# In a linear-attention loop, ScalarE scales the fourth output tile one step later and rounds phi between relu and exponential

## The chip, the core and the metric

One Trainium2 chip, one core. The metric is the device time of one execution of the program, in microseconds (us). Below, PE is the matmul engine (TensorE), DVE is VectorE, ACT is ScalarE, POOL is GpSimd, and SP issues the transfers (DMA) between device memory and on-chip memory.

## The reference, cut to what matters

Six stages act on x (4 sequences of 1024 tokens, 256 features): quantised linear layer, linear attention, quantised linear layer, routed MLP, softmax attention, routed MLP. Only the second is touched:

```python
q = hidden_states @ Wq.T + bq        # 16 heads of 128
k = hidden_states @ Wk.T + bk        # 4 key heads
v = hidden_states @ Wv.T + bv
sq = elu_plus_one(q)                 # phi
sk = elu_plus_one(k)
kv = jnp.einsum('bhsd,bhse->bhde', sk, v)
qkv = jnp.einsum('bhsd,bhde->bhse', sq, kv)
k_sum = sk.sum(axis=2)
norm = jnp.einsum('bhsd,bhd->bhs', sq, k_sum)
attn = qkv / (norm[..., None] + EPS)
return attn @ Wo.T                   # added to x
```

## The kernel before, in words

`linear_attention_phase` first folds kv and Wo of a head into one matrix `m` (128 x 258: 256 output features, then the key sum). Then its loop takes one step `t` for each half sequence (512 tokens, `CH`) of each head: 32 steps (`LOOP`) a sequence, 128 in all, with 16 steps ahead of them for the keys of the first sequence. Every fp32 product is made of three matmuls of rounded parts, high x high, high x low, low x high (`split3`, lines 35 to 37), so each operand exists as a high part, rounded by ACT, and a low part, the difference, made by DVE or POOL.

A query step `t` runs so. PE makes the query of step t (six matmuls of 512 columns) in a bank of PSUM. ACT takes relu(-(q + bias)) (line 1210) and exp(-that) (line 1213); DVE joins both to phi in `f[:, t % 2]` (line 1320, below "the query step of DVE"). In step t + 1 ACT rounds phi into `ph` (line 1202) and POOL makes the low part `pl` (line 1142). In step t + 2 (`LAG` = 2) PE makes the four output tiles of 128 tokens (twelve matmuls of 258 columns), ACT copies their norm columns (line 1219), DVE takes the reciprocal `rnorm` (line 1328) and adds three scaled tiles into x (line 1332), ACT scales the fourth into `ybuf` (line 1239), and POOL adds it to x in the step after (line 1148).

Each engine runs one written list, step by step, and only semaphores tie the lists together. ACT's list in a step before the change: round phi of t - 1; evict the results of step t - 1 (`evict`, `act_evict`); relu and exponential of t; norm columns; key part (lines 1224, 1226, 1232); background work; scale the fourth tile of this step, which waits for this step's reciprocal; round the next piece of wo (line 1246). DVE's list: evictions; key part (1259, 1315); layer norm of the next sequence and background work; the query step; reciprocal; three tiles. POOL's list: low part of phi of t - 1 (1142); addition of the fourth tile (1148); low part of the keys (1152); splits of wq (1128, 1131), of wo (1159) and of MLP weights (568, 570); background work.

The background work is that of the neighbouring stages (quantised layer, routed MLP, layer norm and transposition for softmax attention) of sequences that are ready; `Plan` gives each of its pieces a step. All results of PE go through eight banks of PSUM, taken in turn: a step takes one for the query, four for the outputs, and one for each key, wo or background job, five to seven in all. Before PE writes a bank it waits until the result eight claims earlier has been taken (`wait_emptied`); for the fourth output tile that is the count of `s_y3`, which line 1239 raises.

The loop ends in a barrier, after which softmax attention begins.

Of the kernel before, what the change touches and what calls it, by code (L numbers as in the profile page):

```python
# [4 lines left out]
F32 = mybir.dt.float32  # L5
F32R = mybir.dt.float32r
BF16 = mybir.dt.bfloat16
ALU = mybir.AluOpType
ACT = mybir.ActivationFunctionType
AX = mybir.AxisListType  # L10

P = 128
B, S, D = 4, 1024, 256
# [8 lines left out]
TC = CH // P  # L22
# [877 lines left out]
LAG = 2  # L900
# [40 lines left out]
def linear_attention_phase(nc, sh, c, a):  # L941
# [17 lines left out]
    with ExitStack() as ctx:  # L959
        def sb(name, shape, dt):  # L960
            return ctx.enter_context(nc.sbuf_tensor(f"li_{name}", shape, dt))
# [4 lines left out]
        def sem(name):  # L966
            return sh.sem(f"li_{name}")
# [8 lines left out]
        f = sb("f", [P, 2, CH], F32)  # L976
        ph, pl = pair("phi", [P, LAG + 1, CH])
# [10 lines left out]
        bias_in = sb("bias_in", [P, H], F32)  # L988
        bias = sb("bias", [P, 2, H], F32)
        norm = sb("norm", [P, TC], F32)  # L990
        rnorm = sb("rnorm", [P, TC], F32)
        ybuf = sb("ybuf", [P, 2, D], F32)
        raw = sb("raw", [P, 2, D], F32)
        ps = ctx.enter_context(nc.psum_tensor("li_ps", [P, 8, CH], F32))
# [11 lines left out]
        s_q, s_uq, s_eq, s_f, s_ph, s_pl, s_y, s_norm, s_rn, s_x, s_y3, s_x3 = (sem(n) for n in (  # L1006
            "q", "uq", "eq", "f", "ph", "pl", "y", "norm", "rn", "x", "y3", "x3"))
# [14 lines left out]
        def q_step(t):  # L1022
            return 0 <= t < END

        def y_step(t):
            return LAG <= t < END + LAG
# [90 lines left out]
        @block.gpsimd  # L1117
        def _(pool):
            pool_constants(nc, pool, c, s_const)
            n = 0  # L1120

            def split_wq(hh):
                par = hh % 2
                pool.wait_ge(s_wq[par], 16 * (hh // 2) + 16)
                if hh >= 2:
                    pool.wait_ge(s_q, 2 * hh - 2)
                    pool.wait_ge(s_wq_kept[par], 32 * (hh // 2))
                nc.gpsimd.tensor_tensor(wqh[:, par, :], wq_raw[:, par, :], c.zero.to_broadcast([P, KT * HD]),
                                        ALU.add).then_inc(s_wqh, 1)
                pool.wait_ge(s_wqh, hh + 1)  # L1130
                nc.gpsimd.tensor_tensor(wql[:, par, :], wq_raw[:, par, :], wqh[:, par, :].bitcast(F32),
                                        ALU.subtract).then_inc(s_wql, 1)

            pool.wait_ge(s_bias_in, 16)
            nc.gpsimd.tensor_tensor(bias[:, 0, :], c.zero.to_broadcast([P, H]), bias_in[:], ALU.subtract).then_inc(s_bias, 1)
            nc.gpsimd.tensor_tensor(bias[:, 1, :], bias_in[:], c.one.to_broadcast([P, H]), ALU.add).then_inc(s_bias, 1)
            split_wq(0)
            for t in range(BEGIN, plan.end):
                if q_step(t - 1):
                    k = t - 1  # L1140
                    pool.wait_ge(s_ph, k + 1)
                    nc.gpsimd.tensor_tensor(pl[:, k % (LAG + 1), :], f[:, k % 2, :], ph[:, k % (LAG + 1), :].bitcast(F32),  # L1142
                                            ALU.subtract).then_inc(s_pl, 1)
                if y_step(t - 1):
                    m = t - 1 - LAG
                    pool.wait_ge(s_y3, m + 1)
                    x = x_tile_of(m, 3)
                    nc.gpsimd.tensor_tensor(x, ybuf[:, m % 2, :], x, ALU.add).then_inc(s_x3, 1)
                if t - 3 in kv_time:
                    k, v, i = kv_time[t - 3]  # L1150
                    pool.wait_ge(s_kvh, k + 1)
                    nc.gpsimd.tensor_tensor(kvl[:, i, 0:2 * PK], z[:, k % 3, :], kvh[:, i, 0:2 * PK].bitcast(F32),
                                            ALU.subtract).then_inc(s_kl, 1)
                if t % 2 == 0 and 0 <= t < 2 * H - 2:
                    split_wq(t // 2 + 1)
                if made_time.get(t + 1, 2 * KVH) < 2 * KVH:
                    i = made_time[t + 1]
                    pool.wait_ge(s_woh, i + 1)
                    nc.gpsimd.tensor_tensor(wol[:], wo_raw[:], woh[:].bitcast(F32), ALU.subtract).then_inc(s_wol, 1)
                for part, v in mlp_pieces(c, t):  # L1160
                    pool.wait_ge(s_raw[n % 2], 16 * (n // 2) + 16)
                    split_mlp(nc, pool, c, part, v, raw[:, n % 2, :])
                    nc.gpsimd.sem_inc(s_split, 1)
                    n += 1
                if t - LOOP * (t // LOOP) == 3 and t // LOOP + 1 < B:
                    ln_rstd(nc, pool, sh, ln, t // LOOP + 1, TB, TB)
                pool_background(nc, pool, sh, c, t)

        @block.scalar
        def _(act):  # L1170
# [26 lines left out]
                nc.scalar.activation(kvl[:, t, 2 * PK:KROW], c.zero.to_broadcast([P, 2]), ACT.Copy).then_inc(s_ones, 1)  # L1197
            act.wait_ge(s_small, 64)
            for t in range(BEGIN, plan.end):
                if q_step(t - 1):  # L1200
                    act.wait_ge(s_f, t)
                    nc.scalar.activation(ph[:, (t - 1) % (LAG + 1), :], f[:, (t - 1) % 2, :], ACT.Copy).then_inc(s_ph, 1)  # L1202
                evict(t)
                act_evict(nc, act, c, t)
                if q_step(t):
                    act.wait_ge(s_q, t + 1)
                    act.wait_ge(s_bias, 2)
                    if t >= 2:
                        act.wait_ge(s_pl, t - 1)
                    nc.scalar.activation(f[:, t % 2, :], c.own_bank(("QUERY", t)), ACT.Relu, scale=-1.0,  # L1210
                                         bias=bias[:, 0, t // 2 % H:t // 2 % H + 1]).then_inc(s_uq, 1)
                    act.wait_ge(s_uq, t + 1)
                    nc.scalar.activation(f[:, t % 2, :], f[:, t % 2, :], ACT.Exp, scale=-1.0).then_inc(s_eq, 1)
                if y_step(t):
                    act.wait_ge(s_y, t - LAG + 1)
                    if t > LAG:
                        act.wait_ge(s_rn, t - LAG)
                    for own, banks in out_banks(t - LAG):
                        last = nc.scalar.activation(norm[:, own], ps[:, banks, D], ACT.Copy, bias=ATT_EPS)
                    last.then_inc(s_norm, 1)  # L1220
                if t - 1 in kv_time:
                    k, v, i = kv_time[t - 1]
                    act.wait_ge(c.taken, by_dve["KV", v, i])
                    nc.scalar.activation(ekk[:, k % 2, :], z[:, k % 3, 0:PK], ACT.Relu, scale=-1.0).then_inc(s_ek, 1)
                    act.wait_ge(s_ek, 2 * k + 1)
                    nc.scalar.activation(ekk[:, k % 2, :], ekk[:, k % 2, :], ACT.Exp, scale=-1.0).then_inc(s_ek, 1)
                if t - 2 in kv_time:
                    k, v, i = kv_time[t - 2]
                    act.wait_ge(s_phik, k + 1)
                    if i == 0:  # L1230
                        old_sums(act, v)
                    nc.scalar.activation(kvh[:, i, 0:2 * PK], z[:, k % 3, :], ACT.Copy).then_inc(s_kvh, 1)
                act_background(nc, act, c, t)
                if y_step(t):
                    m = t - LAG
                    act.wait_ge(s_rn, m + 1)
                    if m >= 2:
                        act.wait_ge(s_x3, m - 1)
                    nc.scalar.activation(ybuf[:, m % 2, :], c.own_bank(("OUT", m, 3))[:, 0:D], ACT.Copy, scale=rnorm[:, 3:4]).then_inc(s_y3, 1)
                if made_time.get(t + 1, 2 * KVH) < 2 * KVH:  # L1240
                    i = made_time[t + 1]
                    act.wait_ge(s_wo, 16 * i + 16)
                    if i:
                        act.wait_ge(s_wo_kept, 32 * i)
                        act.wait_ge(c.made, made("MADE", (i - 1) // 2, (i - 1) % 2))
                    nc.scalar.activation(woh[:], wo_raw[:], ACT.Copy).then_inc(s_woh, 1)

        @block.vector
        def _(dve):
# [58 lines left out]
            for t in range(BEGIN, plan.end):  # L1308
# [13 lines left out]
                if y_step(t):  # L1322
                    m = t - LAG
                    dve.wait_ge(s_norm, m + 1)
                    if m:
                        dve.wait_ge(s_y3, m)
                        dve.wait_ge(s_x, 3 * m)
                    nc.vector.reciprocal(rnorm[:], norm[:]).then_inc(s_rn, 1)
                    dve.wait_ge(s_rn, m + 1)
                    for j in range(3):  # L1330
                        x = x_tile_of(m, j)
                        nc.vector.scalar_tensor_tensor(x, c.own_bank(("OUT", m, j))[:, 0:D], rnorm[:, j:j + 1], x, ALU.mult, ALU.add).then_inc(s_x, 1)

        @block.tensor
        def _(pe):
# [578 lines left out]
```

## Time and profile before

| | |
|---|---|
| time, median of 3 runs | 3566.72 us (3566.16 to 3567.49) |
| the profiled execution, its own time | 3566.82 us |
| its span in the profile | 3565.1 us |
| granted PE clock over the span | 0.975 of full speed |
| PE busy over the span | 3348.6 us (94%) |
| DVE busy | 2672.2 us (75%) |
| ACT busy | 2046.0 us (57%) |
| POOL busy | 1054.5 us (30%) |

Busy time is that in which an engine has an instruction in work; matmuls are pipelined, so PE's is not PE at its peak. A line number (L1320) is that of the kernel before. A small part of the matmul records is missing from the trace.

### The profile page before, as it was taken

The page shows a single profiled execution, that of the slowest core. Times are in us where ns is not written, and L with a number is a line of the kernel's source. Part 1 is how long each engine was busy: PE and PEld are TensorE (multiplying, and loading weights), DVE is VectorE, ACT ScalarE, POOL GpSimd, SP SyncE. Part 2 cuts the span into 40 slices and gives each one's busy share as a digit, 9 for nine tenths or more (in the row PEclk, how much of TensorE's full clock was granted, in tenths as well). Part 3 has the DMA queues.
Part 4 walks back from the last instruction along what each step waited for, and adds up shares of the span by engine and source line. Part 5 has one row for each costly group of instructions (what it writes and reads, how often), then busy time and mean ns, then how long its engine had stood idle before and what let it go on. Part 6 is the DMA issues. An engine that isn't in the chain of part 4 may idle for free.

```text
span 3565.1 us, 52686 instructions
## 1 busy us (share of the span) xinstructions
PE 3348.6 (94%) x19398; PEld 2866.0 (80%) x19398; DVE 2672.2 (75%) x4945; ACT 2046.0 (57%) x3911; POOL 1054.5 (30%) x1261
## 2 busy tenths in 40 slices
PE   1799999979999999999999999999999999999993
PEld 1678878868888888888888888888888888888882
DVE  4688797767886787876788677886788767876764
ACT  2577766746556556556555655556555565556551
POOL 3586666642212121222111222212212221122103
PEclk7899999999999999999999999999999999999995
DMA  2121112210000000000000001001000000000001
GB/s 81 56 78 54 60 57 68 66 39 14 14 18 28 17 13 13 14 23 28 13 14 13 27 20 37 14 14 27 23 13 16 19 29 26 13 25 23 26 7 30
DMA packets 98526, 104.21 MB, mean 29 GB/s; under 512 B 10337, under 2 KB 88801, under 8 KB 98145
## 3 DMA queue, kind: packets, MB, share of 16 engines
q1 hardware_dynamic: 98272, 100.85, 9.3%
q8 instruction: 157, 2.57, 0.3%
q14 instruction: 97, 0.79, 0.1%
HBM read 87.18 MB, written 13.63 MB: 28 GB/s over the span
## 4 chain that ended last, share of the span: by engine, by line
PE 68%; DVE 6%; ACT 3%; issue 1%; DMA 0%; POOL 0%; DVEq 0%; SPq 0%; POOLq 0%; ACTq 0%
PE at_ps_job L1807 11%; PE at_ps_job L35 7%; PE at_ps_job L37 6%; PE at_ps_job L36 6%; PE at_ps_o L35 6%; PE at_ps_o L37 6%; PE at_ps_o L36 6%; PE at_ps_s L37 6%; PE at_ps_s L35 6%; PE at_ps_s L36 6%; DVE at_neg_max L1739 1%; ACT x_resident L1673 1%; DVE at_probT_lo L1684 1%; PE at_ps_job L865 1%; DVE at_oT_lo L1715 0%
## 5 line engine op out<-in xcount | busy, mean ns | idle before, releaser
L1630 ACT ACTIVATE at_probT_hi<-at_ps_job 128x512 fp32r<-128x512 f32 x1024 | 610.6, 597 | 898.4 <-PE at_ps_job L1807 895.6
L1684 DVE TENSOR_TENSOR at_probT_lo<-at_ps_job,at_probT_hi 128x512 fp32r<-128x512 f32 x1024 | 703.9, 687 | 278.1 <-ACT at_probT_hi L1630 267.1
L1673 ACT ACTIVATE x_resident<-at_ps_s,at_neg_max 128x1024 f32<-128x1024 f32 x512 | 570.6, 1115 | 149.3 <-DVE at_neg_max L1739 143.3
L1739 DVE TENSOR_REDUCE at_neg_max<-at_ps_s 128x1 f32<-128x1024 f32 x512 | 623.3, 1217 | 6.3
L1807 PE MATMUL at_ps_job<-ident,x_resident 128*128 128x128 f32 x4096 | 613.8, 272 | 5.0 <-DVE at_probT_lo L1684 3.2
L1807 PEld LDWEIGHTS at_ps_job<-ident,x_resident 128*128 128x128 f32 x4096 | 496.2, 140 | 98.9 <-issue 7.5
L35 PE MATMUL at_ps_o<-at_probT_hi,at_v_lo 128*128 128x512 f32 x1024 | 447.2, 437 | 8.5 <-DVE at_oT_lo L1715 7.3
L1613 POOL TENSOR_TENSOR at_w_hi<-at_w_raw,ch_cols 128x256 fp32r<-128x256 f32 x192 | 117.6, 613 | 1121.9 <-PE at_ps_job L37 1100.9
L35 PE MATMUL at_ps_s<-at_k_hi,at_q_lo 128*128 128x512 f32 x1024 | 445.7, 435 | 0.0
L37 PE MATMUL at_ps_s<-at_k_lo,at_q_hi 128*128 128x512 f32 x1024 | 405.0, 396 | 0.0
L37 PE MATMUL at_ps_o<-at_probT_lo,at_v_hi 128*128 128x512 f32 x1024 | 404.5, 395 | 0.0
L36 PE MATMUL at_ps_s<-at_k_hi,at_q_hi 128*128 128x512 f32 x1024 | 402.8, 393 | 0.0
L36 PE MATMUL at_ps_o<-at_probT_hi,at_v_hi 128*128 128x512 f32 x1024 | 402.0, 393 | 0.0
L1697 DVE SCALAR_TENSOR_TENSOR x_resident<-at_ps_job,at_row_inv,x_resident 128x256 f32<-128x256 f32 x512 | 223.7, 479 | 24.9 <-PE at_ps_job L37 11.4
L37 PEld LDWEIGHTS at_ps_s<-at_k_lo,at_q_hi 128*128 128x128 f32 x1024 | 192.0, 187 | 44.7
L37 PEld LDWEIGHTS at_ps_o<-at_probT_lo,at_v_hi 128*128 128x128 f32 x1024 | 192.1, 188 | 44.2
L35 PEld LDWEIGHTS at_ps_o<-at_probT_hi,at_v_lo 128*128 128x128 f32 x1024 | 193.4, 189 | 39.0 <-issue 17.0
L1142 POOL TENSOR_TENSOR li_phi_lo<-li_f,li_phi_hi 128x512 fp32r<-128x512 f32 x128 | 166.0, 1297 | 177.3 <-ACT li_phi_hi L1202 175.9
L35 PE MATMUL at_ps_job<-ch_xnT_hi,at_w_lo 128*128 128x512 f32 x512 | 203.3, 397 | 11.1 <-POOL at_w_lo L1615 10.1
L36 PEld LDWEIGHTS at_ps_s<-at_k_hi,at_q_hi 128*128 128x128 f32 x1024 | 194.3, 190 | 23.9
L35 PEld LDWEIGHTS at_ps_s<-at_k_hi,at_q_lo 128*128 128x128 f32 x1024 | 193.4, 189 | 23.5
L36 PEld LDWEIGHTS at_ps_o<-at_probT_hi,at_v_hi 128*128 128x128 f32 x1024 | 194.5, 190 | 21.6
(274 smaller groups left out, 7500.2 us busy)
## 6 DMA issues: line engine op xcount, KB each, us to landing
at_w_raw<-attn_w SPq DMA_DIRECT2D x256, 128.0 KB, 2.3
at_w_raw<-mlp_w SPq DMA_DIRECT2D x112, 128.0 KB, 2.3
li_wo_hi<-li_wo_kept SPq DMA_DIRECT2D x24, 256.0 KB, 2.6
li_wo_lo<-li_wo_kept SPq DMA_DIRECT2D x24, 256.0 KB, 2.9
li_wq_hi<-li_wq_kept SPq DMA_DIRECT2D x48, 128.0 KB, 2.2
li_wq_lo<-li_wq_kept SPq DMA_DIRECT2D x48, 128.0 KB, 2.5
x_resident<-x SPq DMA_DIRECT2D x4, 1024.0 KB, 10.6
out<-x_resident SPq DMA_DIRECT2D x4, 1024.0 KB, 5.7
```

Source lines behind the costliest of these rows:

```text
L35: nc.tensor.matmul(out, al, bh, start=start, stop=False)
L36: nc.tensor.matmul(out, ah, bh, start=False, stop=False)
L37: return nc.tensor.matmul(out, ah, bl, start=False, stop=stop)
L865: nc.tensor.matmul(out[:, k * P:(k + 1) * P], c.tiles[:, j, k * P:(k + 1) * P], c.hot[:, j, :], start=(j == 0), stop=(j == TB - 1))
L1142: nc.gpsimd.tensor_tensor(pl[:, k % (LAG + 1), :], f[:, k % 2, :], ph[:, k % (LAG + 1), :].bitcast(F32), ALU.subtract).then_inc(s_pl, 1)
L1613: nc.gpsimd.tensor_tensor(hi, src, none, ALU.add).then_inc(s_wh[part], 1)
L1630: nc.scalar.activation(ph[:, i // TC, 4 * half:4 * half + 4, (i % TC) * P:(i % TC + 1) * P], c.turned_bank(2 * TB * u + 2 * i + half), ACT ...
L1673: nc.scalar.activation(prob[:, slot % 2, :], ps_s[slot % 2][:], ACT.Exp, bias=nmax[:, slot:slot + 1], accum_out=rsum[:, u % 2, slot:slot + ...
L1684: nc.vector.tensor_tensor(pl[at], c.turned_bank(2 * TB * u + 2 * i + half), ph[at].bitcast(F32), ALU.subtract).then_inc(s_pl, 1)
L1697: last = nc.vector.scalar_tensor_tensor(x, src[:, j * D:(j + 1) * D], rinv[:, v % 2, tile:tile + 1], x, ALU.mult, ALU.add)
L1739: nc.vector.tensor_reduce(nmax[:, slot:slot + 1], ps_s[slot % 2][:], AX.X, ALU.max, negate=True).then_inc(s_max, 1)
L1807: last = nc.tensor.transpose(turned[:, j, :], prob[:, i % 2, kt * P:(kt + 1) * P], sh.ident[:])
```

## The change

ACT's list is put in another order. Phi of step t - 1 is no longer rounded at the head of step t, ahead of the evictions, but between relu and exponential of step t. The scaling of the fourth tile moves from the end of its own step to the next step, behind that step's exponential and ahead of its norm columns. So `rnorm` gets two halves, used in turn, and DVE's reciprocal waits for the scaling of two steps earlier, not for that of the step before. POOL adds the fourth tile one step later. No instruction is added or removed.

```diff
-        rnorm = sb("rnorm", [P, TC], F32)
+        rnorm = sb("rnorm", [P, 2, TC], F32)
...
-                if y_step(t - 1):
-                    m = t - 1 - LAG
+                if y_step(t - 2):
+                    m = t - 2 - LAG
                     pool.wait_ge(s_y3, m + 1)
                     x = x_tile_of(m, 3)
                     nc.gpsimd.tensor_tensor(x, ybuf[:, m % 2, :], x, ALU.add).then_inc(s_x3, 1)
...
-                if q_step(t - 1):
-                    act.wait_ge(s_f, t)
-                    nc.scalar.activation(ph[:, (t - 1) % (LAG + 1), :], f[:, (t - 1) % 2, :], ACT.Copy).then_inc(s_ph, 1)
                 evict(t)
                 act_evict(nc, act, c, t)
...
                     nc.scalar.activation(f[:, t % 2, :], c.own_bank(("QUERY", t)), ACT.Relu, scale=-1.0,
                                          bias=bias[:, 0, t // 2 % H:t // 2 % H + 1]).then_inc(s_uq, 1)
+                if q_step(t - 1):
+                    act.wait_ge(s_f, t)
+                    nc.scalar.activation(ph[:, (t - 1) % (LAG + 1), :], f[:, (t - 1) % 2, :], ACT.Copy).then_inc(s_ph, 1)
+                if q_step(t):
                     act.wait_ge(s_uq, t + 1)
                     nc.scalar.activation(f[:, t % 2, :], f[:, t % 2, :], ACT.Exp, scale=-1.0).then_inc(s_eq, 1)
+                if y_step(t - 1):
+                    m = t - 1 - LAG
+                    act.wait_ge(s_rn, m + 1)
+                    if m >= 2:
+                        act.wait_ge(s_x3, m - 1)
+                    nc.scalar.activation(ybuf[:, m % 2, :], c.own_bank(("OUT", m, 3))[:, 0:D], ACT.Copy,
+                                         scale=rnorm[:, m % 2, 3:4]).then_inc(s_y3, 1)
...
-                if y_step(t):
-                    m = t - LAG
-                    act.wait_ge(s_rn, m + 1)
-                    if m >= 2:
-                        act.wait_ge(s_x3, m - 1)
-                    nc.scalar.activation(ybuf[:, m % 2, :], c.own_bank(("OUT", m, 3))[:, 0:D], ACT.Copy, scale=rnorm[:, 3:4]).then_inc(s_y3, 1)
...
-                    if m:
-                        dve.wait_ge(s_y3, m)
-                        dve.wait_ge(s_x, 3 * m)
-                    nc.vector.reciprocal(rnorm[:], norm[:]).then_inc(s_rn, 1)
+                    if m >= 2:
+                        dve.wait_ge(s_y3, m - 1)
+                        dve.wait_ge(s_x, 3 * m - 3)
+                    nc.vector.reciprocal(rnorm[:, m % 2, :], norm[:]).then_inc(s_rn, 1)
```

## Rows read from the trace of the kernel before

**Rows 1.** Windows, the steady part of the loop: busy us (instructions) per engine, granted clock.
```profile
125.00:746.00 621.00, 575.46 (x3359) 496.31 (x3357) 510.92 (x1129) 438.51 (x1013) 425.51 (x413) 0.97 0.20 62
```

**Rows 2.** Chain that ended last, behind the barrier: start, us, what.
```profile
749.10 4.86 DMA at_w_raw<-attn_w
```

**Rows 3.** Windows, six stretches with much DVE work: the first, and the sum.
```profile
138.00:184.00 46.00, 36.32 (x174) 29.87 (x175) 41.64 (x78) 30.13 (x68) 38.02 (x35) 0.88 0.20 63
...
sum 242.00, PE 207.50 PEld 172.63 DVE 227.79 ACT 161.49 POOL 181.31; mean PE 34.58 PEld 28.77 DVE 37.97 ACT 26.92 POOL 30.22
```

**Rows 4.** Windows, five stretches with little DVE work: the sum.
```profile
sum 268.00, PE 261.95 PEld 231.91 DVE 188.22 ACT 201.05 POOL 178.41; mean PE 52.39 PEld 46.38 DVE 37.64 ACT 40.21 POOL 35.68
```

**Rows 5.** Waits, 125 to 746 us: who waited for whom, total us, times, longest.
```profile
POOL li_phi_lo L1142 <- ACT li_phi_hi L1202: 175.9, 90, 4.5
ACT li_ybuf L1239 <- DVE li_rnorm L1328: 126.4, 94, 5.5
...
PE li_ps L35 <- DVE li_f L1320: 29.4, 27, 2.9
...
PE li_ps L35 <- POOL li_wo_lo L1159: 5.4, 5, 2.2
```

**Rows 6.** Timeline of ACT: start, duration, engine, line, operation.
```profile
576.41 0.47 ACT L1239 ACTIVATE li_ybuf<-li_ps,li_rnorm 128x256 f32<-128x256 f32 x1 [0.78 <-DVE li_rnorm L1328]
576.79 0.62 ACT L1202 ACTIVATE li_phi_hi<-li_f 128x512 fp32r<-128x512 f32 x1
577.31 0.68 ACT L1210 ACTIVATE li_f<-li_ps,li_bias 128x512 f32<-128x512 f32 x1
578.02 0.63 ACT L1213 ACTIVATE li_f<-li_f 128x512 f32<-128x512 f32 x1
...
649.77 0.62 ACT L1202 ACTIVATE li_phi_hi<-li_f 128x512 fp32r<-128x512 f32 x1
650.84 0.69 ACT L1210 ACTIVATE li_f<-li_ps,li_bias 128x512 f32<-128x512 f32 x1 [0.45 <-PE li_ps L37]
```

**Rows 7.** Timeline of DVE.
```profile
181.88 0.16 DVE L1328 RECIPROCAL li_rnorm<-li_norm 128x4 f32<-128x4 f32 x1
...
575.54 0.75 DVE L1320 SCALAR_TENSOR_TENSOR li_f<-li_ps,li_bias,li_f 128x512 f32<-128x512 f32 x1 [1.00 <-ACT li_f L1213]
576.21 0.17 DVE L1328 RECIPROCAL li_rnorm<-li_norm 128x4 f32<-128x4 f32 x1
576.41 1.27 DVE L1332 SCALAR_TENSOR_TENSOR x_resident<-li_ps,li_rnorm,x_resident 128x256 f32<-128x256 f32 x3
578.68 0.75 DVE L1320 SCALAR_TENSOR_TENSOR li_f<-li_ps,li_bias,li_f 128x512 f32<-128x512 f32 x1 [1.00 <-ACT li_f L1213]
...
717.68 0.17 DVE L1328 RECIPROCAL li_rnorm<-li_norm 128x4 f32<-128x4 f32 x1
```

**Rows 8.** Timeline of PE.
```profile
657.02 0.36 PE L35 MATMUL li_ps<-ch_r_rounded 128*128 128x256 f32 x1 [1.94 <-DVE x_resident L1332]
...
699.62 0.40 PE L36 MATMUL li_ps<-ch_xnT_hi,li_wq_hi 128*128 128x512 f32 x1
...
700.78 0.29 PE L35 MATMUL li_ps<-li_m_hi,li_phi_lo 128*128 128x258 f32 x1
...
702.24 0.39 PE L35 MATMUL li_ps<-li_wo_hi,li_kvT_lo 128*128 128x512 f32 x1
```

**Rows 9.** Timeline of POOL.
```profile
577.48 1.29 POOL L1142 TENSOR_TENSOR li_phi_lo<-li_f,li_phi_hi 128x512 fp32r<-128x512 f32 x1
...
656.20 0.72 POOL L570 TENSOR_TENSOR ch_r_rounded<-li_raw,ch_r_rounded 128x256 fp32r<-128x256 f32 x1
...
723.00 1.29 POOL L1142 TENSOR_TENSOR li_phi_lo<-li_f,li_phi_hi 128x512 fp32r<-128x512 f32 x1 [2.00 <-ACT li_phi_hi L1202]
```

**Rows 10.** DVE's layer-norm line: durations in ns, least, median, most.
```profile
L170 DVE TENSOR_SCALAR li_xn<-x_resident,ln_mean,ln_rstd x24: 403/1348/1534, 150.4 to 503.7; 128x256 f32<-128x256 f32 x24
```

**Rows 11.** Timeline of DVE, two layer-norm instructions of a step.
```profile
723.12 2.07 DVE L170 TENSOR_SCALAR ch_r<-x_resident,ln_mean,ln_rstd 128x256 f32<-128x256 f32 x2
```

More of the change, by code:

```diff
@@ L1331, in _ @@
                         x = x_tile_of(m, j)
-                        nc.vector.scalar_tensor_tensor(x, c.own_bank(("OUT", m, j))[:, 0:D], rnorm[:, j:j + 1], x, ALU.mult, ALU.add).then_inc(s_x, 1)
+                        nc.vector.scalar_tensor_tensor(x, c.own_bank(("OUT", m, j))[:, 0:D], rnorm[:, m % 2, j:j + 1], x, ALU.mult, ALU.add).then_inc(s_x, 1)
         @block.tensor
```

## Prediction, made before the change was run

> **What bounds the kernel now.** The diff touches only the linear-attention phase, so I first asked the windows view how long its loop is and who works in it. The 127 steps whose reciprocals I can time lie inside 125 to 746 us, 621 of 3565 us; PE is busy 575 us, DVE 511, ACT 439, POOL 426 [rows 1]. So the most that this edit can reach is a sixth of the run. What is saved there reaches the end: the attention phase starts behind a barrier with a load of its own from device memory, and the chain that ended last hangs on that load and not on anything that could have started sooner [rows 2].
>
> Second, windows over stretches with DVE's layer-norm and ranking work, and over stretches without. In six stretches (138 to 184, 225 to 274, 305 to 347, 447 to 506, 556 to 574 and 714 to 742 us), together 242 us and some 46 steps, DVE is busy 227.8 us, 94%, and PE 207.5 [rows 3]. In five others (186 to 212, 276 to 304, 366 to 446, 576 to 656, 658 to 712), 268 us, PE is busy 262 us and DVE 188 [rows 4]. The loop is thus DVE's in a good third and PE's in most of the rest, and ACT leads almost nowhere. The longest wait of ACT, 126.4 us for the reciprocal, costs by itself nothing; PE's wait for DVE's query step is 29.4 us in 27 waits, and that is what a better order could shorten [rows 5].
>
> Third, one light step. ACT waits for the reciprocal at 576.21, scales the fourth tile at 576.41, rounds phi at 576.79, does relu at 577.31 and the exponential at 578.02 [rows 6]; DVE's query step starts at 578.68, 3.14 us after the one before at 575.54 [rows 7]. The chain is 0.67 + 0.20 + 0.38 + 0.52 + 0.71 + 0.66 = 3.14 us, and twelve of the periods between reciprocals are 3.13 to 3.17 us (the first begins at 181.88, the last ends at 717.68) [rows 7].
>
> **Part 1: the chain.** After the edit the step is query step, phi, exponential, query step. Phi can start when the query step is written, 0.75 + 0.04 us on; the exponential 0.52 behind it, 0.63 long, and DVE starts 0.03 after: 1.97 us instead of 3.14 [rows 6, 7]. What is late next is DVE itself: 0.67 + 0.20 + three tiles of 1.27 less the overlap of 0.08, 2.06 us [rows 7]. And PE: six query matmuls at 0.232 (five spacings are 1.16) and twelve output matmuls, 1.46 us, make 2.85 us [rows 8]. PE is the later, so a light step falls from 3.14 to 2.85, 0.29 us. For twelve steps: -3.5 us. Bounds: 0, since several of the twelve lie where PE runs without a gap, and 12 x 1.08 = -13 us where DVE alone sets the pace. I take PE's value, as the nearest rows are PE's.
>
> **Part 2: when POOL works.** Phi's low part on POOL starts at 577.48, 1.94 us after the query step's start [rows 7, 9]. Behind the edit it can start at 0.79 + 0.62 + 0.07 = 1.48 us, 0.46 sooner, wherever relu was done early, that is in DVE's stretches. This matters because DVE and POOL stretch each other: the layer-norm instruction takes 403 ns at least and 1348 at the median [rows 10], and two of them next to POOL's phi of 723.00 take 2.07 us [rows 9, 11]. If POOL is done 0.46 sooner, DVE is free that much sooner. In the first two stretches POOL is itself nearly full (38 of 46 us in the first [rows 3]), and nothing moves; about 30 steps are left. Bounds 0 and 30 x 0.46 = -14 us; I take 0.3 a step, -9 us, nearer the full shift, since an instruction that meets POOL waits for the rest of POOL's instruction. The Trainium skill, in SBUF — State Buffer, SBUF: two separate sides, says that VectorE and GpSimd share a port pair as an exclusive lock that the first holds for its whole instruction. By that rule the sum for these steps would be the full -14 us, by the rows' spread less; the trace agrees with the lock as such (403 against 1348 ns).
>
> **Part 3: phi between relu and exponential.** Relu to exponential is 0.71 us now, since the second needs the first's result. With phi between it is about 0.58 + 0.52 = 1.10 us (0.58 is relu's 0.68 less the overlap of 0.10 that phi's 0.62 and its 0.52 to the next show) [rows 6]. In DVE's stretches relu is early and this is hidden behind DVE's background work. Where PE leads, the query step comes 0.39 us later after its matmuls; PE needs it only a step later, after 2.85 us and more, so it is hidden too, until DVE gets a heavy step: then DVE starts that 0.39 late. There are about eight such changes: +3 us (bounds 0 and 6).
>
> **Part 4: what now queues behind relu.** Relu waits for PE's query matmuls and for the evictions ahead of it, and phi waits behind relu. Where PE leads, phi, its low part on POOL and all that POOL has listed behind it (the fourth tile's addition, the key's low part, the splits of wq, wo and MLP weights) move later. One place is visible: PE's MLP matmul of 657.02 starts when POOL's split of 656.20 ends (656.92; the tile named as releaser was long done) [rows 8, 9], and POOL had begun that list straight after phi. There phi ran at 649.77 and relu, late for PE's sake, at 650.84 [rows 6]; behind relu phi would run at 651.42, so POOL starts some 1.6 us later: +1.6. For wo the two effects oppose: ACT's rounding of wo no longer stands behind the wait for the reciprocal, POOL's part stands behind a later phi. PE waits for wo's low part 5.4 us in five waits [rows 5]; bounds -5 and +5, and I take 0. Together +2 us.
>
> **Part 5: at nothing.** The fourth tile's scaling ends at about 0.79 + 0.52 + 0.53 + 0.47 = 2.3 us after the query step's start, against 1.3 now. Its bank is wanted by a later job of PE, which first waits for DVE's third tile (0.67 + 0.20 + 1.27 = 2.14) and runs an output tile of 0.36; that is the cover. Without it, 0.2 us in some 40 steps with key jobs, +8 us. The second half of rnorm takes away a wait of DVE that never shows. POOL's addition one step later finds its input ready, as before. SP's transfers stay where they are; they follow POOL's splits. The last phi no longer waits behind a scaling: -0.4.
>
> **Sum.** -3.5 - 9 + 3 + 2 - 0.4 = -7.9, call it -8. The profiled execution took 3566.8 us with a span of 3565.1, beside a median of 3566.7, so both bases agree: 3558.7 us.
>
> **Rivals.** *A, nothing to measure.* The shorter chain lands where PE is full, and POOL's shift only moves the collision to another instruction of DVE. For: PE busy 262 of 268 us [rows 4]. Against: PE still waits 29.4 us for the query step [rows 5]. Part 1 gives 0, part 2 a third (-3), losses +2: 3566.
>
> *B, slower.* Phi too late in PE's stretches. After the query matmuls: relu 0.05, phi 0.58 behind, 0.62 long, 0.07 to POOL, 1.29 there: 2.6 us. PE comes to the output matmuls that need it after 1.46 + 1.39 = 2.85 us [rows 8, 9]. So 0.25 us are left in a step without jobs, and it decides as soon as POOL is held for more than that by what it still has from the step before (an addition of 0.74 or a split of 0.72). Ten such places at the 1.6 us of part 4 are +16, less the 8 gained: 3575. Against: most of PE's steps have a job, which adds 0.5 to 1.4 us. The Trainium skill speaks for this rival: PSUM — Partial Sum Buffer, Engine vs sequencer instructions, calls ScalarE's queue strictly first in, first out, so a waiting relu holds phi even if its input lies ready. The trace agrees: rows of ACT follow the program's order with the wait for the reciprocal in front of a phi that was ready.
>
> *C, a larger gain through the clock.* PE's granted clock is 0.97 over the loop and 0.88 in the first stretch, so about 3% x 2 x 621 = 37 us pass at 1.2 GHz, worth up to 18 us of PE's time [rows 1, 3]; it falls after PE has stood waiting. If half of that comes back with shorter waits: 3549.
>
> **How the numbers follow.** My forecast has 0.45, A 0.25, B 0.20, C 0.10. A measurement of this kernel tells about 0.2%, 7 us, from no change. My forecast's own range is 3552 to 3563; 0.06 of its chance lies within 7 us of before, and A leaves 0.03 on the side of faster and 0.02 on that of slower. Faster 0.39 + 0.10 + 0.03 = 0.52, slower 0.20 + 0.02 = 0.22, same 0.06 + 0.20 = 0.26. The range 3546 to 3572 takes C and the nearer half of B.
>
> **What would show it.** After the edit ACT's wait for the reciprocal should be nearly gone and turn into waits for the query step; light steps should have periods near 2.85; phi's low part should start near 1.5 us after the query step in DVE's stretches; the layer-norm median should fall. I am wrong if PE's waits for phi's low part grow by more than 5 us (B), if the sum of PE's waits for the query step stays (A), or if the loop shrinks by over 15 us with a higher clock (C).

## The result

The changed kernel takes 3604.8 us (median of 4 runs, 3601.41 to 3606.47) beside 3567.1 us (4 runs, 3566.16 to 3569.53) of the kernel before on the same chip: ratio 1.0103, 95% interval 1.0086 to 1.0121. It is slower by 37.7 us, outside the predicted range of 3546 to 3572, where 3558.7 was forecast. The profiled execution has a span of 3603.6 us.

### The profile page after: what moved, and what is told of

Read it like the earlier page. It is cut to its first block, busy times and chain, and to the rows that moved or that the text cites. A ratio compares the mean times of both kernels' runs of the same rounds, so it can differ in the third digit from the quotient of the medians.

```text
span 3603.6 us, 52685 instructions
## 1 busy us (share of the span) xinstructions
PE 3352.4 (93%) x19398; PEld 2861.9 (79%) x19398; DVE 2653.8 (74%) x4945; ACT 2034.7 (56%) x3911; POOL 1050.6 (29%) x1261
## 4 chain that ended last, share of the span: by engine, by line
PE 67%; DVE 6%; ACT 3%; issue 1%; DMA 0%; POOL 0%; DVEq 0%; SPq 0%; POOLq 0%; ACTq 0%
PE at_ps_job L1809 11%; PE at_ps_job L35 7%; PE at_ps_job L37 6%; PE at_ps_job L36 6%; PE at_ps_o L35 6%; PE at_ps_o L37 6%; PE at_ps_o L36 6%; PE at_ps_s L37 6%; PE at_ps_s L35 6%; PE at_ps_s L36 6%; DVE at_neg_max L1741 1%; ACT x_resident L1675 1%; DVE at_probT_lo L1686 1%; PE at_ps_job L865 1%; DVE at_oT_lo L1717 0%
```

## The profile after

The loop is the place. Its first reciprocal is at 136.93 us and its last at 783.68 (before: 135.96 and 745.72): 646.75 us instead of 609.76, +37.0. The windows view of the loop up to its end answers to [rows 1] (columns: window, length, then busy us and count of PE, PE's weight loads, DVE, ACT, POOL; granted clock, DMA share, GB/s), and a row of the chain that ended last to [rows 2]:

```profile
125.00:784.00 659.00, 578.31 (x3360) 491.38 (x3358) 493.07 (x1129) 425.67 (x1013) 419.77 (x413) 0.98 0.19 59
```

```profile
787.07 4.94 DMA at_w_raw<-attn_w
```

PE does the same work in nearly the same time, 578 us instead of 575 at a granted clock of 0.98 instead of 0.97, and stands 80.7 us (659 - 578.31) where it stood 45.5 (621 - 575.46). So 35 of the 38 us by which this window is longer are idle time of PE, and the clock has no part in the loss (30.7 us at the lower level, 37.5 before). Even DVE, POOL and ACT are busy for less. The barrier's load follows 37.97 us later than before, 787.07 against 749.10 [rows 2]: nothing behind the loop gives any of it back.

The waits view of the changed kernel, 125 to 785 us (who waited for whom: total us, times, longest), against [rows 5]:

```profile
POOL li_phi_lo L1142 <- ACT li_phi_hi L1211: 229.4, 107, 7.5
ACT li_f L1207 <- PE li_ps L37: 152.7, 114, 6.4
...
PE li_ps L35 <- ACT li_ybuf L1220: 41.6, 51, 3.0
...
PE li_ps L35 <- DVE li_f L1322: 18.3, 16, 3.2
...
PE li_ps L1362 <- ACT li_ybuf L1220: 5.1, 7, 0.7
...
PE li_ps L35 <- DVE x_resident L1334: 3.3, 1, 3.3
```

The third row is new. PE waits 41.6 us in 51 waits for `li_ybuf`, the scaling of the fourth tile; with the rows of other lines of PE's list (L1362 and four smaller ones) it is 51.1 us in 64. Before, this wait was there once, with 0.2 us. The other waits of PE fell at the same time: for the query step from 29.4 to 18.3 us, for phi's low part from 7.6 to 5.7, for wo's low part from 5.4 to 0.8; one for x rose from 1.9 to 3.3. Together, 50.9 - 11.1 - 1.9 - 4.6 + 1.4 = 34.7 us, PE's 35. The second row is almost as telling: ACT's relu waits for PE's query matmuls 114 times in 128 steps. Before, it did so 27 times, because ACT stood 94 times at the scaling, waiting for the reciprocal, ahead of it [rows 5].

One step of the stretch that had been PE's shows how. PE, then ACT of the changed kernel (start, duration, what, and in brackets the idle time before it with its releaser):

```profile
637.00 0.39 PE L37 MATMUL li_ps<-ch_xnT_lo,li_wq_hi 128*128 128x512 f32 x1
...
638.56 0.29 PE L37 MATMUL li_ps<-li_m_lo,li_phi_hi 128*128 128x258 f32 x1
639.57 0.50 PE L35 MATMUL li_ps<-li_wkv_hi,ch_xnT_lo 128*128 128x512 f32 x1 [0.72 <-ACT li_ybuf L1220]
```

```profile
637.43 0.69 ACT L1207 ACTIVATE li_f<-li_ps,li_bias 128x512 f32<-128x512 f32 x1 [2.19 <-PE li_ps L37]
638.01 0.62 ACT L1211 ACTIVATE li_phi_hi<-li_f 128x512 fp32r<-128x512 f32 x1
638.54 0.62 ACT L1214 ACTIVATE li_f<-li_f 128x512 f32<-128x512 f32 x1
639.06 0.46 ACT L1220 ACTIVATE li_ybuf<-li_ps,li_rnorm 128x256 f32<-128x256 f32 x1
```

The last query matmul ends at 637.39. Relu starts 0.04 later, and behind it come phi, exponential and at last the scaling, which ends at 639.52. PE's twelve output matmuls are over at 638.85, and its next job wants the bank of that very tile: a step with one query, four outputs and two jobs takes seven banks, and this is the eighth claim. PE stands 0.72 us, in this step and the same in the steps on both sides. The period here is 5.96 us (reciprocals at 639.86 and 645.82) where it had been 4.96. That is 1.00 us for a recorded wait of 0.72: before, the job's first matmul began 0.12 us after the start of the last output matmul and its second 0.23 later, here 1.01 and 0.34. The idle time in the record is thus less than the wait costs.

What the edit was to bring is there too, where steps are light. DVE of the changed kernel:

```profile
725.42 0.16 DVE L1330 RECIPROCAL li_rnorm<-li_norm 128x4 f32<-128x4 f32 x1
...
727.46 0.17 DVE L1330 RECIPROCAL li_rnorm<-li_norm 128x4 f32<-128x4 f32 x1
```

This step takes 2.04 us where it took 3.14. But of the twelve such periods five fell below 2.85, and three rose above 3.9. Layer norm on DVE, the first two rows of its line in the changed kernel, the second against [rows 10] (durations in ns, least/median/most):

```profile
L170 DVE TENSOR_SCALAR ch_r<-x_resident,ln_mean,ln_rstd x40: 385/408/1369, 145.8 to 771.9; 128x256 f32<-128x256 f32 x40
L170 DVE TENSOR_SCALAR li_xn<-x_resident,ln_mean,ln_rstd x24: 402/824/1386, 152.1 to 518.9; 128x256 f32<-128x256 f32 x24
```

Its median fell from 1348 to 824 ns (that of the first row from 759 to 408), so DVE does meet POOL less there. It is not there that the time was lost. Of the 127 periods between reciprocals, the 47 that began in DVE's six stretches take 3.1 us less than before, together, and the other 80 take 40.1 us more.

## The experiments

Two theories. **T1**: the scaling, behind the exponential, keeps the fourth tile's bank from PE. **T2**: phi behind relu is late, with all that POOL has queued behind it. The first four kernels ran beside 15 runs of before (median 3566.56 us, 3564.08 to 3568.41), the second four beside 9 (3565.96 us, 3564.38 to 3568.57).

### e2: phi alone

The edit, in ACT's list of the kernel before:

```diff
-                if q_step(t - 1):
-                    act.wait_ge(s_f, t)
-                    nc.scalar.activation(ph[:, (t - 1) % (LAG + 1), :], f[:, (t - 1) % 2, :], ACT.Copy).then_inc(s_ph, 1)
                 evict(t)
                 act_evict(nc, act, c, t)
...
                                          bias=bias[:, 0, t // 2 % H:t // 2 % H + 1]).then_inc(s_uq, 1)
+                if q_step(t - 1):
+                    act.wait_ge(s_f, t)
+                    nc.scalar.activation(ph[:, (t - 1) % (LAG + 1), :], f[:, (t - 1) % 2, :], ACT.Copy).then_inc(s_ph, 1)
+                if q_step(t):
                     act.wait_ge(s_uq, t + 1)
                     nc.scalar.activation(f[:, t % 2, :], f[:, t % 2, :], ACT.Exp, scale=-1.0).then_inc(s_eq, 1)
```

> The kernel before, with one part of the change: phi is rounded between relu and exponential; the fourth tile is scaled at the end of its own step as before. Theory T1 (the loss comes from the fourth tile's PSUM bank, which PE wants back before ACT, held by relu's wait for the query matmuls, has scaled it): no such wait here, 3567 us, within 5 of before. Rival T2 (the loss comes from phi and its low part on POOL, late behind relu): all of the loss stays, 3595 to 3605 us.

Measured: 3587.5 us (3586.45 to 3589.48), ratio 1.0058 (1.0043 to 1.0073), +21. It lies between the two expectations: phi's place costs much, but does not explain all. By the same periods as above its loop is 21.8 us longer, 1.7 of them in DVE's stretches and 20.1 outside. The waits of PE in it, 125 to 769 us:

```profile
PE li_ps L35 <- DVE li_f L1321: 34.0, 32, 3.2
PE li_ps L35 <- POOL li_phi_lo L1142: 14.1, 15, 2.5
PE li_ps L35 <- POOL li_wo_lo L1159: 5.9, 5, 2.2
```

Phi's low part is missed for 14.1 us in 15 waits where it was 7.6 in 6, the query step for 34.0 instead of 29.4 [rows 5]. PE's wait for `li_ybuf` is 2.0 us. POOL's phi starts 3.17 us (median) behind DVE's query step, where it had been 1.94.

### e3: the scaling alone

The changed kernel, with phi back at the head of the step:

```diff
+                if q_step(t - 1):
+                    act.wait_ge(s_f, t)
+                    nc.scalar.activation(ph[:, (t - 1) % (LAG + 1), :], f[:, (t - 1) % 2, :], ACT.Copy).then_inc(s_ph, 1)
                 evict(t)
                 act_evict(nc, act, c, t)
...
                                          bias=bias[:, 0, t // 2 % H:t // 2 % H + 1]).then_inc(s_uq, 1)
-                if q_step(t - 1):
-                    act.wait_ge(s_f, t)
-                    nc.scalar.activation(ph[:, (t - 1) % (LAG + 1), :], f[:, (t - 1) % 2, :], ACT.Copy).then_inc(s_ph, 1)
-                if q_step(t):
                     act.wait_ge(s_uq, t + 1)
                     nc.scalar.activation(f[:, t % 2, :], f[:, t % 2, :], ACT.Exp, scale=-1.0).then_inc(s_eq, 1)
```

> The changed kernel with phi put back to the head of the step; only the scaling is one step late, behind the exponential. T1: relu to exponential is 0.71 us and the scaling follows 0.52 later, so the bank comes free about 0.4 us sooner after the query matmuls than in the changed kernel; PE's gap of 1.0 us falls to 0.6, and about 20 us of PE's wait for the scaling stay: 3585 to 3592 us. T2: phi is early again, 3560 to 3570 us.

Measured: 3573.52 us (10 runs, 3571.55 to 3576.8), ratio 1.002 (1.001 to 1.0029), +7. T1 had wanted 3585 or more, so alone it doesn't stand either; the time lies nearer T2's span. Yet PE does wait for the scaling, 125 to 750 us:

```profile
PE li_ps L35 <- ACT li_ybuf L1219: 28.7, 53, 3.0
PE li_ps L35 <- DVE li_f L1321: 14.4, 12, 2.5
```

28.7 us in 53 waits, 33.4 in 66 with the other lines. The net is only +7 because something else gains (phi early: the query step is missed for 14.4 us instead of 29.4). The two halves alone give +21 and +7, the whole +37.7: some 10 more than their sum. With phi ahead of it the scaling comes yet later, and each of PE's waits grows from 0.54 (28.7 / 53) to 0.82 us (41.6 / 51).

### e5 and e6: the scaling one place earlier, one later

Both start from the changed kernel. e5 puts the scaling of t - 1 between phi and exponential; e6 puts the same block behind the norm columns (behind `last.then_inc(s_norm, 1)`). The diff of e5:

```diff
                 if q_step(t - 1):
                     act.wait_ge(s_f, t)
                     nc.scalar.activation(ph[:, (t - 1) % (LAG + 1), :], f[:, (t - 1) % 2, :], ACT.Copy).then_inc(s_ph, 1)
+                if y_step(t - 1):
+                    m = t - 1 - LAG
...
                 if q_step(t):
                     act.wait_ge(s_uq, t + 1)
                     nc.scalar.activation(f[:, t % 2, :], f[:, t % 2, :], ACT.Exp, scale=-1.0).then_inc(s_eq, 1)
-                if y_step(t - 1):
-                    m = t - 1 - LAG
...
```

> The changed kernel with the scaling one place earlier, between phi and exponential. T1: the bank comes free 0.52 us sooner in every step that PE leads, at 50 to 60 such waits 25 us back, less some 4 us for an exponential 0.37 later where DVE leads: 3580 to 3588 us. T2: phi is as late as in the changed kernel, 3600 to 3608 us.

> The changed kernel with the scaling one place later, behind the norm columns, which first wait for PE's output tiles. T1: the suspected cost goes up; the bank comes free 0.15 to 0.4 us later in each of 50 to 60 steps, 3612 to 3628 us. T2: phi is where it was, 3600 to 3608 us.

Measured: e5 3578.22 us (3576.65 to 3578.94), ratio 1.0031 (1.0019 to 1.0044); e6 3610.32 us (3607.37 to 3613.83), ratio 1.0122 (1.0107 to 1.0137). One exponential earlier gives back 27 us, and PE's wait goes from 41.6 us in 51 to 14.2 in 37; e5 lies just below T1's span and far below T2's. Behind the norm columns the scaling costs 5.5 us more than in the changed kernel, with a wait of 49.3 us in 60. That time lies between the two spans and settles nothing; the wait went T1's way. The rows of the wait, e5 (125 to 757 us), then e6 (125 to 787 us):

```profile
PE li_ps L35 <- ACT li_ybuf L1217: 14.2, 37, 1.7
```

```profile
PE li_ps L35 <- ACT li_ybuf L1227: 49.3, 60, 3.0
```

### e8 and e7: phi at the head, the scaling one step late but early in the list

e8 starts from the kernel before, with `rnorm`, POOL's addition and DVE's waits as in the change; ACT scales the tile of t - 1 behind the evictions, ahead of relu. e7 has the same block between relu and exponential. The diff of e8 in ACT's list:

```diff
                 evict(t)
                 act_evict(nc, act, c, t)
+                if y_step(t - 1):
+                    m = t - 1 - LAG
+                    act.wait_ge(s_rn, m + 1)
+                    if m >= 2:
+                        act.wait_ge(s_x3, m - 1)
+                    nc.scalar.activation(ybuf[:, m % 2, :], c.own_bank(("OUT", m, 3))[:, 0:D], ACT.Copy,
+                                         scale=rnorm[:, m % 2, 3:4]).then_inc(s_y3, 1)
...
-                if y_step(t):
-                    m = t - LAG
-                    act.wait_ge(s_rn, m + 1)
...
```

> Phi at the head of the step, then the evictions, then the scaling of the step before, then relu and exponential. Nothing of the scaling hangs on the query matmuls, phi starts 0.5 us sooner after the query step than before, and the evictions no longer stand behind the wait for the reciprocal: PE's wait for the scaling near 0, POOL's phi 1.5 us after the query step, 3552 to 3562 us, faster than before. If phi's earlier start is worth nothing, 3564 to 3570 us.

> Phi at the head of the step as before; the fourth tile's scaling, one step late, stands between relu and exponential. If the changed kernel loses by two things, the bank that waits for the scaling behind relu and exponential, and phi behind relu: phi is early here, and the scaling ends 0.05 + 0.58 + 0.47 = 1.1 us after the query matmuls, before PE's 1.46 us of output matmuls are over, so PE's wait for the scaling falls under 10 us. 3557 to 3565 us. If a late scaling costs by its step and not by that wait, 3573 us as with phi at the head and the scaling behind the exponential.

Measured: e8 3546.3 us (3541.99 to 3547.34), ratio 0.994 (0.9927 to 0.9952); e7 3546.91 us (3544.59 to 3549.26), ratio 0.9945 (0.9932 to 0.9957). Both beat the kernel before by 19 to 20 us, more than was expected of them. These are the fastest kernels of the study. e8's windows row for its loop (first reciprocal at 137.22, last at 725.83):

```profile
125.00:726.00 601.00, 562.45 (x3362) 489.05 (x3360) 497.51 (x1131) 439.96 (x1012) 426.43 (x413) 0.98 0.21 65
```

Between the first and last reciprocal the loop takes 588.6 us instead of 609.8. Of these 21.2 us PE's idle time gives 6.8 and its busy time 14.4: the clock record of the profiled execution has 17.1 us at the lower level in this stretch of e8 and 37.5 before. By an estimate from these two figures, 20.4 us less at 1.2 GHz give back up to 10 us. So part of e8's gain goes with the clock, as rival C had it, though in another kernel; the size of that part isn't isolated by any run. The waits, first of e7 (125 to 728 us), then of e8 (125 to 726 us):

```profile
PE li_ps L35 <- ACT li_ybuf L1217: 7.3, 7, 1.6
```

```profile
ACT li_phi_hi L1202 <- DVE li_f L1321: 100.5, 89, 5.1
...
PE li_ps L35 <- ACT li_ybuf L1210: 5.7, 6, 1.7
```

Here ACT, freed from the reciprocal, does stand at the query step, ahead of relu; relu's own wait for PE is 22.5 us in 32.

Three things follow. From e8 to e3 only the scaling moves, from ahead of relu to behind the exponential, and this costs 27 us, beside 23 us more of PE's wait for it (5.7 to 28.7). From e7 to e3 it moves past the exponential alone, and the cost is the same 27: between relu and exponential it is just in time (7.3 us in 7 waits), behind it it is late 53 times. And relu to exponential takes 0.93 us (median) in e7 and 0.72 in e8, while the times differ by 0.6 us: an exponential 0.2 us late costs nothing that shows.

Five places of the scaling can be put in one table. Taken is the distance from the last query matmul to the scaling's end (relu 0.04 behind the matmuls, then the starts of the list), less PE's cover of 1.46 us; beside it is the mean of PE's seven waits at line 1361 or 1362, all in like steps:

| kernel | relu to scaling, its length | end behind the matmuls | less 1.46 | mean wait there | period, 4.96 before |
|---|---|---|---|---|---|
| e7 | 0.58 + 0.47 | 1.09 | -0.37 | 0.2, once | 4.96 |
| e5 | 1.11 + 0.46 | 1.61 | 0.15 | 1.5 / 7 = 0.21 | 5.44 |
| e3 | 1.26 + 0.46 | 1.76 | 0.30 | 2.5 / 7 = 0.36 | 5.57 |
| changed | 1.63 + 0.46 | 2.13 | 0.67 | 5.1 / 7 = 0.73 | 5.96 |
| e6 | 1.68 + 0.47 | 2.19 | 0.73 | 5.6 / 7 = 0.80 | 6.08 |

The wait is the lateness plus 0.06 to 0.07 us in all four kernels that have it; 0.05 of that is the time from the scaling's end to the start of PE's matmul (639.52 to 639.57). That settles what the wait of PE is. The last column is the median of four periods, the one shown above and those beside it. Where PE waits, it grows by 0.25 to 0.32 us more than the wait, as in the step shown.

### e4: the bank's wait taken away, phi left behind relu

The changed kernel, with the scaling of t - 1 ahead of relu:

```diff
                 evict(t)
                 act_evict(nc, act, c, t)
+                if y_step(t - 1):
+                    m = t - 1 - LAG
...
                     act.wait_ge(s_uq, t + 1)
                     nc.scalar.activation(f[:, t % 2, :], f[:, t % 2, :], ACT.Exp, scale=-1.0).then_inc(s_eq, 1)
-                if y_step(t - 1):
-                    m = t - 1 - LAG
...
```

> The changed kernel with only the scaling moved, ahead of relu and behind the evictions; phi stays between relu and exponential. With the bank theory, PE's wait for the scaling goes, and the cost of the late phi stays as in the kernel with phi alone moved: 3583 to 3592 us, PE's wait for the scaling under 5 us. If the bank wait is only where PE's idleness shows and not its cause, 3600 us and more.

Measured: 3588.09 us (3585.6 to 3588.85), ratio 1.0059 (1.0045 to 1.0073), as expected: 17 us under the changed kernel. PE's waits for the scaling are 3.5 us in 5. e4 and e8 differ only in phi's place, and by 42 us.

But e5, in which PE waits for the scaling for 14.2 us in 37, is 10 us faster than e4. ACT's waits in e4 (125 to 767 us) show what an early place costs when phi is late:

```profile
ACT li_ybuf L1207 <- POOL x_resident L1148: 74.0, 54, 4.3
ACT li_ybuf L1207 <- DVE li_rnorm L1330: 62.4, 33, 3.6
```

The scaling writes a half of `ybuf` that POOL must have added to x before. POOL makes phi's low part ahead of that addition, so a late phi makes the addition late; the scaling waits for it, and relu, phi and exponential wait behind the scaling. In e8, with phi at the head, this wait is 4.6 us in 3. The 42 us are thus the price of phi behind the scaling and relu together, not of phi behind relu alone.

One step of DVE's stretches shows part of it: first e8, then e4, each with DVE's query step, its key part, the next query step, and POOL's phi:

```profile
538.52 0.74 DVE L1321 SCALAR_TENSOR_TENSOR li_f<-li_ps,li_bias,li_f 128x512 f32<-128x512 f32 x1
...
541.16 0.42 DVE L1316 SCALAR_TENSOR_TENSOR li_z<-li_z,li_ekk 128x256 f32<-128x256 f32 x1
...
543.39 0.74 DVE L1321 SCALAR_TENSOR_TENSOR li_f<-li_ps,li_bias,li_f 128x512 f32<-128x512 f32 x1
...
540.01 1.30 POOL L1142 TENSOR_TENSOR li_phi_lo<-li_f,li_phi_hi 128x512 fp32r<-128x512 f32 x1 [1.56 <-ACT li_phi_hi L1202]
```

```profile
564.61 0.74 DVE L1322 SCALAR_TENSOR_TENSOR li_f<-li_ps,li_bias,li_f 128x512 f32<-128x512 f32 x1
...
567.25 1.44 DVE L1317 SCALAR_TENSOR_TENSOR li_z<-li_z,li_ekk 128x256 f32<-128x256 f32 x1
...
570.47 0.74 DVE L1322 SCALAR_TENSOR_TENSOR li_f<-li_ps,li_bias,li_f 128x512 f32<-128x512 f32 x1
...
567.12 1.29 POOL L1142 TENSOR_TENSOR li_phi_lo<-li_f,li_phi_hi 128x512 fp32r<-128x512 f32 x1 [1.48 <-ACT li_phi_hi L1218]
```

It is the same step of the program in both. In e8 POOL's phi starts 1.49 us behind the query step and is over (541.31) as DVE's key part comes; that takes 0.42 us. In e4 it starts 2.51 us behind, 0.13 ahead of the key part, which takes 1.44. The step lasts 4.87 us in e8 and 5.86 in e4. Over all, e4's periods are 12.8 us longer than e8's in DVE's stretches and 28.4 outside. PE misses phi's low part for 18.0 us in 26 waits (e8: 5.8 in 4) and the query step for 28.8 (e8: 21.7). All of PE's idle time in the loop is 62.1 us in e4 and 38.6 in e8.

### e10: phi behind the exponential

In ACT's list of the kernel before:

```diff
-                if q_step(t - 1):
-                    act.wait_ge(s_f, t)
-                    nc.scalar.activation(ph[:, (t - 1) % (LAG + 1), :], f[:, (t - 1) % 2, :], ACT.Copy).then_inc(s_ph, 1)
                 evict(t)
                 act_evict(nc, act, c, t)
...
                     act.wait_ge(s_uq, t + 1)
                     nc.scalar.activation(f[:, t % 2, :], f[:, t % 2, :], ACT.Exp, scale=-1.0).then_inc(s_eq, 1)
+                if q_step(t - 1):
+                    act.wait_ge(s_f, t)
+                    nc.scalar.activation(ph[:, (t - 1) % (LAG + 1), :], f[:, (t - 1) % 2, :], ACT.Copy).then_inc(s_ph, 1)
```

> The kernel before with phi moved behind the exponential instead of between relu and exponential; the scaling as before. The exponential comes 0.39 us sooner than with phi between, phi and POOL's low part about 0.7 us later. If phi alone costs its 21 us by the lateness of POOL's low part (PE's wait for it, and the collision with DVE's instructions): 3592 to 3602 us. If it costs them by the later exponential: 3567 to 3578 us.

Measured: 3587.03 us (3586.44 to 3589.25), ratio 1.0057 (1.0041 to 1.0072), the same as e2 and neither of what was expected. The exponential is not late here (0.72 us behind relu; 1.09 in e2), and the loss is no smaller. e7 against e8 shows no cost of a later exponential either, and e5 beats e4 with one 0.37 us later. So e2's loss is most likely that of its later phi; e10 alone doesn't show it, since its phi is later still. That a phi yet later costs no more is made of two opposite parts. PE misses its low part longer (125 to 769 us):

```profile
PE li_ps L35 <- POOL li_phi_lo L1142: 28.5, 33, 3.9
PE li_ps L35 <- DVE li_f L1320: 17.5, 13, 3.2
```

and DVE meets POOL less: its key part takes 539 ns in the mean over the 56 in the loop, against 946 in e2 and 826 before. POOL's phi starts 4.51 us behind the query step, past the key part. A new wait comes in as well: relu itself waits for POOL's low part, whose input it overwrites, for 15.3 us in 18 waits (e2: 4.3 in 2). So the sum does not rise with the lateness alone.

## Why the prediction was wrong, step by step

**Part 1** held in kind. Where DVE alone sets the pace the period is 2.04 us, beside 2.06 worked out for DVE. But the twelve light periods together fell by 1.2 us, not 3.5, since some grew; in e8 they only fall from 3.14 to 3.06 (median), less than the 0.29 booked. The term is small either way.

**Part 2** failed first in order, though by itself it cost little. The clause at fault is that phi would start 0.46 us sooner "wherever relu was done early, that is in DVE's stretches". I never showed that relu stays early there. It had waited for PE in 2 of the 47 steps of these stretches, 0.7 us; in the changed kernel it waits in 37 of them, 44.4 us. POOL's phi starts within 1.7 us of the query step in 8 of the 47 and in 5 of the other 81; the median in the stretches is 3.46 us and over all 3.95, not 1.48. Relu's wait had been short because ACT stood at the reciprocal before it came to relu [rows 5]; with that wait gone, relu waits 114 times. Instead of -9 the stretches gave -3.1, all causes together.

With phi left at the head the shift does come: in e8 the median is 1.50 us, 28 of the 47 steps are within 1.7, and the stretches are 13.8 us shorter. That this is the POOL effect alone isn't shown, for the steps outside gain 7.3 us as well and the clock has its part. The lock named there is seen again: the same 128x256 instruction of DVE takes 0.42 or 1.44 us beside POOL's 1.29. By the rule of the Trainium skill (SBUF — State Buffer, SBUF: two separate sides) DVE waits out the whole instruction that holds the port pair; the trace agrees roughly, as 567.25 + 1.44 = 568.69 lies 0.28 us past POOL's end at 568.41. A full wait and then the free 0.42 would end 0.14 later, and spans on POOL are rough.

**Parts 3 and 4** had the right sign and were far too small: +3 and +2 beside +21 for phi's place alone (e2). The later exponential, Part 3's term, came out as worked out (relu to exponential 1.11 us, against 1.10), and no run shows a cost of it. What was mis-sized is Part 4's late phi. For wo it had bounds of -5 and +5 and took 0; PE's wait for it fell by 4.6 us. Rival B is this mechanism, and at 3575 was nearest of all cases; I priced it at ten places of 1.6 us. Against it I put that most of PE's steps have a job; but of the waits for phi's low part there are 15 and 26 in e2 and e4, and 20.1 us of e2's loss lie outside DVE's stretches, which is where this rival put it. The strict order of ACT's queue, which the Trainium skill states (PSUM — Partial Sum Buffer, Engine vs sequencer instructions), spoke for B. The trace agrees: in 99 of the 114 waits of relu, DVE's query step, the input of the phi behind it, is written before relu starts.

**Part 5**, "at nothing", is the other failure, and about as large: with the scaling one place earlier the changed kernel gets back 27 us (e5), with phi at the head 31 (e3). The scaling was placed "2.3 us after the query step's start", a distance measured from DVE, and so its cover was DVE's third tile. In PE's stretches the scaling hangs on something else: it is queued behind relu, which waits for PE's own query matmuls, and ends 2.13 us behind them (637.39 to 639.52). PE's cover is its twelve output matmuls, 1.46 us. The pieces of both stood in Part 1 and rival B (relu 0.05 behind the matmuls, phi 0.58 behind relu; 1.46), yet were not set against each other: 0.67 us is missing, and PE waited 0.72. The bound given, 0.2 us in some 40 steps, +8, was too low for the same reason: it is 51.1 us in 64 waits. The price of this place is 27 us with phi at the head (e8 to e3).

**The split of the +37.7** by kernels: phi's place +21 (e2), the scaling's one step later, behind the exponential, +7 net of what phi's earlier start gives back (e3), and some +10 for the two in series. It isn't a sum of independent parts: phi between relu and exponential costs 21 us with the scaling at the end of its step (e2), 31 with it behind the exponential (e3 to changed) and 42 with it ahead of relu (e8 to e4). What phi's lateness costs by way of DVE's collisions and what by way of PE's waits isn't settled in full: in e2 DVE's stretches hold 1.7 us of the loss, and the waits of PE for the query step, for phi's low part and for wo rise by 11.6 us of 21; in e10 the parts are others with the same sum. A kernel in which POOL's phi is late and touches nothing of DVE's wasn't tried.

**The signs named in advance.** ACT's wait for the reciprocal did vanish (126.4 to 0.2 us); it turned into waits for PE's query matmuls (152.7) and not for the query step (13.4), which is where the forecast order and the real one part. PE's waits for phi's low part did not grow in the whole change (5.7 us): PE was late itself, for the scaling, and hid them. This sign of rival B therefore failed in the very kernel in which phi was late, and showed only in e2 and e4. Rival C's clock didn't save the changed kernel: 0.98 and the loop 37 us longer. In e8's profiled execution it has a part in the gain.

## What to carry to other kernels

When a wait is taken out of an in-order queue, look for what the next instruction in it waits for: a wait that the trace shows as short may be short only because the engine stood somewhere else first. When a step that frees a bank is moved, work out its end from every engine that can be in the lead, and set it against the time at which the bank is claimed in that case; behind an instruction that waits for PE, the cover is only what PE has left to do after the result waited for. And try the parts of an edit apart: here half of it, in another order, was worth 20 us. Even a good place for one part can be a bad one beside the other, as e4 against e5 shows.

## What was not expected of the hardware

Part 3 had this from single rows, and the runs bear it out. ACT starts a 128x512 instruction 0.52 to 0.53 us after the one before if it doesn't need its result (638.01 to 638.54, with 0.62 us for each), and 0.72 after it if it does (median from relu to exponential in e3 and e8). So phi between relu and exponential adds only 0.37 us to that distance (0.72 to 1.09 in e2), not its 0.52.

Unexpected was how sharp the edge of a collision of DVE and POOL is. In the two steps shown, the key part of 128x256 takes 0.42 us when POOL's phi ends 0.15 us behind its start (541.16 and 541.31), and 1.44 us when POOL's starts 0.13 us ahead of it (spans on POOL are rough). POOL came 1.02 us later after the query step, and the step became 0.99 us longer.
